# Layer 3 of a decoder: the mixture's routing moved from a phase of its own into the rounds of the cross attention before it

## The reference, cut to what matters

```python
x = x + jnp.tanh(g_xattn[3]) * _L3_xattn_ref(_layernorm(x, axis=-1), ctx_2048, ...)
x = x + jnp.tanh(g_ffn[3]) * _L3_ffn_ref(_layernorm(x, axis=-1), L3_ffn_Wg, L3_ffn_w1, L3_ffn_w2)

def _moe_forward(x, Wg, w1, w2):            # S = 4096 tokens, E = 8 experts, K = 2, C = 1280
    probs = jax.nn.softmax(xr @ Wg, axis=-1)
    gate_vals, expert_idx = jax.lax.top_k(probs, K)
    flat_e = expert_idx.reshape(-1)
    oh = jax.nn.one_hot(flat_e, E, dtype=jnp.int32)
    pos = jnp.sum((jnp.cumsum(oh, axis=0) - 1) * oh, axis=1)   # rank of a choice within its expert
    kept = pos < C
    ...                                     # rows gathered per expert, relu(x w1) w2, weighted sum
```

## Time and profile before

| | us |
|---|---|
| median of 3 runs (lowest, highest) | 3552.48 (3547.12, 3557.26) |
| the profiled execution: time | 3538.33 |
| the profiled execution: span | 3536.3 |
| mean granted TensorE clock, share of full | 0.898 |
| PE, DVE, ACT, POOL busy | 2850.8, 2150.4, 1478.8, 1097.6 |

### The profile page before, as it was taken

How to read it: one execution, slowest core, us unless ns; L and a number is a source line. 1 busy time by engine, 2 the same in 40 slices (tenths; PEclk the granted TensorE clock), 3 DMA queues, 4 the chain that set the end, 5 groups by cost and what they waited for, 6 DMA issues and landing times. The chain is left out here.

```text
span 3536.3 us, 59953 instructions
## 1 busy us (share of the span) xinstructions
PE 2850.8 (81%) x20178; PEld 1824.3 (52%) x20178; DVE 2150.4 (61%) x4916; ACT 1478.8 (42%) x3032; POOL 1097.6 (31%) x1466
## 2 busy tenths in 40 slices
PE   5488887565899994679946798999989839999995
PEld 4233335222555553433323586454558628888884
DVE  7699995676677775734468686888868740000003
ACT  5377774254232224589935454222235302221120
POOL 3211111475233335412289442000034360111111
PEclk7599997798999997589969899999989759999997
DMA  8866644599422223678400341000034321211114
GB/s 270 202 115 120 122 100 141 212 363 344 138 82 81 78 81 138 165 140 117 86 1 1 136 145 58 1 1 1 1 117 143 103 74 37 77 60 57 57 58 146
DMA packets 261546, 386.11 MB, mean 109 GB/s; under 512 B 56801, under 2 KB 188878, under 8 KB 260992
## 3 DMA queue, kind: packets, MB, share of 16 engines
q1 hardware_dynamic: 226064, 301.49, 32.0%
q0 software_dynamic: 25152, 68.22, 5.6%
q10 hardware_dynamic: 10032, 12.58, 1.0%
HBM read 227.49 MB, written 160.24 MB: 110 GB/s over the span
## 5 line engine op out<-in xcount | busy, mean ns | idle before, releaser
L3090 POOL DMA_INDIRECT rows_out<-e_out,e_tr_dest x224 | 234.9, 1049 | 832.0 <-DVE e_out L3690 491.7
L1102 ACT ACTIVATE a_pt<-a_psS 128x512 f32<-128x512 f32 x512 | 277.6, 595 | 106.3 <-PE a_psS L998 101.9
L3690 DVE COPY e_out<-e_psD 128x512 f32<-128x512 f32 x40 | 27.7, 692 | 461.5 <-PE e_psD L3658 461.4
L3445 PE MATMUL e_psG<-e_wgu,e_yT 128*128 x576 | 276.3, 603 | 28.8 <-ACT e_yT L3477 26.3
L1124 DVE TENSOR_REDUCE a_mx_sb<-a_psM 128x4 f32<-128x1024 f32 x256 | 293.1, 1215 | 10.5 <-PE a_psM L981 9.5
L1012 PE MATMUL a_psV<-a_pt,a_vt 128*18 128x256 f32 x4096 | 290.2, 385 | 1.2 <-issue 0.8
L3647 PE MATMUL e_psH<-e_yT,e_w 128*128 128x256 f32 x1280 | 285.4, 381 | 1.6 <-issue 0.8
L3658 PE MATMUL e_psD<-e_w,e_hT 128*128 128x256 f32 x1280 | 282.7, 379 | 0.0
L3588 ACT ACTIVATE e_hT<-e_psH 128x512 f32<-128x512 f32 x160 | 95.5, 597 | 445.7 <-PE e_psH L3647 441.2
L3647 PEld LDWEIGHTS e_psH<-e_yT,e_w 128*128 128x128 f32 x1280 | 244.8, 191 | 35.8 <-issue 2.1
L3658 PEld LDWEIGHTS e_psD<-e_w,e_hT 128*128 128x128 f32 x1280 | 240.2, 190 | 31.1
(11 more groups left out here) (434 smaller groups left out, 6182.9 us busy)
## 6 DMA issues: line engine op xcount, KB each, us to landing
kbd<-e_wd SPq DMA_DIRECT2D x64, 512.0 KB
cr_kbd<-kbd SPq DMA_DIRECT2D x64, 512.0 KB, 3.7
rows_in<-zeros POOLq DMA_DIRECT2D x36, 522.0 KB, 6.4
e_xin<-rows_in SPq DMA_DIRECT2D x144, 128.0 KB
vbd<-e_bd SPq DMA_DIRECT2D x64, 272.0 KB
cr_vbd<-vbd SPq DMA_DIRECT2D x64, 272.0 KB, 2.7
cq_rows<-rows_out SPq DMA_DIRECT2D x32, 512.0 KB, 6.0
e_w<-in_L_ffn_w_dram SPq DMA_DIRECT2D x16, 1024.0 KB, 7.8
```

The costliest lines, as they stand in the source:

```text
L1102: act.activation(pt[:, probs(t, h), b, :, :], psS[:, unit(t, h, b) % S_BANKS, :].rearrange("p (k c) -> p k c", k=KC), ACT.Exp, scale=scale ...
L3090: pool.indirect_dma_start(out=self.rows_out[0:limit, :], out_offset=bass.IndirectOffsetOnAxis(ap=self.dest[:, t:t + 1], axis=0), in_=rows, ...
L3445: ins = pe.matmul(psG[:, u, :], yT[:, u, k, :], wgu[:, e, k, :], start=(k == 0), stop=(k == KC - 1))
```

## The change

`phase_route_scatter` is gone. Its work is a class `Routing3`, whose methods `phase_cross` calls inside its rounds, only in layer 3. Each step runs a fixed number of rounds behind: in round `s` tile s-5 is surveyed, s-9 normed, s-10 turned, s-11 routed; the group whose first tile is s-15 is chosen, with s-16 carried and counted, with s-17 placed; tile s-18 is scattered, 2 DMAs a round. The transposes go to the free columns of `psU`, the logits to `psT`, the counts to `psO`, so PE also waits for those who read or write these banks. The rounds run on to s = 49. The barrier between the phases, and the clearing of semaphores there, are gone; the setup of constants on POOL is in round 2, and the prefetch of expert weights is at tile 8 of the cross attention.

```diff
+class Routing3:
+    SURVEY, NORM, TURN, ROUTE = 5, 9, 10, 11
+    CHOOSE, CARRY, COUNT, PLACE, SEND = 15, 16, 16, 17, 18
...
+    def gpsimd(self, pool, s):
+        g = self.group_at(s, self.SURVEY + G - 1)
+        if g is not None:
+            pool.wait_ge(self.eased, g + 1)
+            pool.tensor_tensor(self.core.rstd[:, self.group(g)], self.vareps[:, self.group(g)], self.core.half[:, 0:G], ALU.pow).then_inc(self.rooted, 1)
+        t = self.tile_at(s, self.SEND)
+        if t is not None:
+            g, j = divmod(t, G)
+            pool.wait_ge(self.placed, g + 1)
+            for k in range(K):
+                pool.indirect_dma_start(out=self.rows_in[:, :], ...).then_inc(self.sent[g % self.RING], 16)
+    def turn(self, pe, s, psU, o_copied):
+        pe.wait_ge(self.y_ready, t + 1)
+        pe.wait_ge(o_copied, min(s - 2, TILES))
+        if t >= 1:
+            pe.wait_ge(self.y_copied, t)
+        for k in range(KC):
+            ins = pe.transpose(psU[:, DIM + k * P:DIM + (k + 1) * P], self.y[...], self.core.ident[:, :])
+    def count(self, pe, s, psO, o_ready):
+        pe.wait_ge(self.masked, g + 1)
+        pe.wait_ge(self.carried, (g + 1) * (G + 1))
+        pe.wait_ge(o_ready, min(s, TILES))
...
@@ phase_cross, tensor @@
-                for s in range(-4, TILES + 3):
+                for s in range(-4, TILES + 3 if routing is None else routing.last):
                     if ok(s + 1):
                         scores(s + 1)
                     if ok(s + 4):
+                            routing.logits_taken(pe, s)
                         turn_y(s + 4)
                     if ok(s):
                         turn_probs(s)
+                        routing.turn(pe, s, psU, o_copied)
                     if ok(s + 3):
                         project(s + 3)
                     if ok(s - 1):
+                            routing.ranks_taken(pe, s)
                         values(s - 1)
+                        routing.route(pe, s, psT, y_copied, sum_copied)
                     if ok(s + 2):
+                            routing.logits_taken(pe, s)
                         sum_squares(s + 2)
                     if ok(s - 2):
+                            routing.turned_out(pe, s)
                         turn_out(s - 2)
                     if ok(s - 3):
                         project_out(s - 3)
+                        routing.count(pe, s, psO, o_ready)
@@ flamingo_decoder @@
-        phase_cross(core, "cr3", kbd[1], vbd[1], turned[0], a["L3_xattn_b_q"], turned[3], a["L3_xattn_b_o"], x_gate(3))
-        core.clear_semaphores()
...
-            phase_route_scatter(core, a["L3_ffn_Wg"], weight, rows_in, 8 * CAPACITY, MARK3, f_gate(3), prefetch)
+            with ExitStack() as c2:
+                routing = Routing3(core, c2, a["L3_ffn_Wg"], weight, rows_in, 8 * CAPACITY, MARK3, f_gate(3), prefetch)
+                phase_cross(core, "cr3", ..., x_gate(3), routing=routing)
```

More of the change, by code:

```diff
@@ L1446, in phase_cross @@
+def phase_cross(core, name, kbd_dram, vbd_dram, wq, bq, wo, bo, gate, prefetch=None, routing=None):
     nc = core.nc
@@ L1518, in _ @@
                         prefetch(sp)
+                    if t == 8 and routing is not None:
+                        routing.sync(sp)
                 load_values(TILES - 2)
@@ L1524, in _ @@
                 pool.memset(ones[:, :], 1.0).then_inc(ones_made, 1)
-                for s in range(-6, TILES + 1):
+                for s in range(-6, TILES + 1 if routing is None else routing.last):
                     t = s + 6
@@ L1651, in _ @@
                     if ok(s + 4):
+                        if routing is not None:
+                            routing.logits_taken(pe, s)
                         turn_y(s + 4)
@@ L1681, in _ @@
                             act.activation(pT[:, t % 2, 4 * r:4 * r + 4, :], psP[:, r, :, :], ACT.Copy).then_inc(p_copied, 1)
+                    if routing is not None:
+                        routing.scalar_turned(act, s, psU)
                     t = s + 1
@@ L1696, in _ @@
                         act.activation(square[:, t:t + 1], psT[:, 1, 0:1], ACT.Copy).then_inc(sum_copied, 1)
+                    if routing is not None:
+                        routing.scalar_logits(act, s, psT, q_summed)
                     t = s - 2
@@ L1707, in _ @@
                 dve.tensor_scalar(bias_out[:, :], bias_out[:, :], gate, None, ALU.mult).then_inc(bias_scaled, 1)
-                for s in range(-6, TILES + 4):
+                for s in range(-6, TILES + 4 if routing is None else routing.last):
+                    if routing is not None:
+                        routing.vector_survey(dve, s, added)
                     if ok(s + 6):
@@ L1721, in _ @@
                         dve.bn_aggr(core.mv[:, t, :], stats[:, t % 2, :]).then_inc(averaged, 1)
+                    if routing is not None:
+                        routing.vector_average(dve, s)
+                        routing.vector_multiply(dve, s, psO)
                     if ok(s + 1):
@@ L1748, in _ @@
                                           ALU.subtract, ALU.mult).then_inc(y_ready, 1)
+                    if routing is not None:
+                        routing.vector(dve, s)
                     if ok(s - 1):
```

474 lines of the change are left out of this document (251 added, 223 removed).

## The result

| | us |
|---|---|
| before, median of 4 runs beside it (lowest, highest) | 3550.3 (3547.12, 3557.26) |
| changed, median of 4 runs | 3507.6 (3500.34, 3513.66) |
| ratio, 95% interval | 0.9878, [0.9861, 0.9895] |
| changed, profiled execution: time, span, mean clock | 3507.26, 3505.5, 0.902 |
| predicted | 3505 (3484 to 3546) |

A forecast was written before the change was run, and what follows sets the result against it. DVE was to bound the attention's rounds, POOL's scatters what follows. Of 119.7 us, 27 for longer rounds and 45 behind the attention leave 47.7 gained: 3552.5 - 47.7 = 3504.8, predicted 3505, range 3484 to 3546.

The forecast's parts named there:

- The bound of the rounds: Layer 3 cross attention: PE's round grows from 5.6 to 6.4 us, DVE's mean to 6.71, so DVE becomes the bound.
- DVE's 6.9 us a round: Rounds 15 to 28: 6.9 us each, between DVE's mean 6.71 and worst round 8.2; 18.5 us added over 14 rounds.
- the stretch: Attention's rounds 5 to 33 together: 27 us longer with the routing inside; lower bound 15, upper 45.
- The clock: PE's clock in the attention's rounds with routing inside: stays at 1.00.
- The rival of the falling clock: Waits lower PE's clock in the rounds: about 11 us each, 57 us more, ending at 3562; chance 0.03.
- Rounds 29 to 34: End of the attention, worked as rounds 29 to 33 with two `place`, one `choose`, one `carry_on`: 5.5 us longer.
- POOL in the rounds: From round 18 two scatters a round, 2.56 us, fit in the 2.66 us that POOL idles.
- The tail: From round 34's output projection to the last scatter's end: 45 us, between 41 and 46, upper bound 50.
- the starving of POOL: Behind the attention POOL may wait for group 5's `place`; DVE's 8.6 us a group otherwise keeps ahead of 10.2 of scatters.
- Late steps in the rounds: Rival: scatters in rounds 18 to 33 delay hand-overs and `place`, 64 us more, ending at 3569; chance 0.11.
- Waits adding up: Rival: DVE's group work adds to PE's rounds, about 8.3 us each in 15 to 28, ending at 3530; chance 0.19.
- The rule on the shared port: DVE steps sharing ports with GpSimd could wait out a scatter; predicted norm at worst 0.25 us late, sum unchanged.

The follow-up runs named there:

- experiments 3: Changed kernel with DVE's norm for the router done twice, the second into a spare tile; one run, 3527.9 us.
- experiment 4: Changed kernel with the two transposes per tile for the router done twice on PE; one run, 3518.9 us.
- experiment 5: Changed kernel repeated (3505.6 us); variants of it: count in `psT` instead of the output bank 3504.4, norm on ACT instead of DVE 3495.8, both 3500.8.
- experiment 2: Changed kernel without the 32 scatters of groups 4 to 7, those after the attention; one run, 3485.6 us.
- experiment 1: Changed kernel without the 32 scatters of groups 0 to 3, those beside the attention's rounds; one run, 3504.4 us.
- experiment 6: Changed kernel with scatters of groups 4 to 7 dropping all rows but index 0 (3505.2 us), or replaced by chained memsets (3494.4 us); one run each.

## Why the prediction was right, and where its terms were off

*The bound of the rounds.* Right. PE's round without DVE in the way came out at 6.34 us where 6.4 was worked out (rounds 11 to 14: 25.36, forecast 4 x 6.3), and the doubled transposes cost 0.22 a round there. The logits' four records took 0.61 us from first start to last end, not 0.45, and the round did not show it. That DVE, not PE, would be the bound from round 15 on is right only in part: PE was the busier of the two, and without the clock's share 4.5 us more on DVE cost 3.3 and 3.0 us more on PE cost 1.6 (experiments 3 and 4).

*DVE's 6.9 us a round.* Measured 7.17; the stretch 100.3 us, forecast 14 x 6.9 = 96.6. Of the 3.7 us between them 2.7 are the half-clock round. Without it a round is 6.97 us: DVE's own sum was 6.49, below the 6.71 of the working, and the waits took 0.48 over it where 0.2 had been given, so two misses nearly cancel. The working had named the place, the count that waits for the division of its own round; experiment 5 prices it at 2.0 us over fourteen rounds, besides the clock. (In the working, 14 x (6.9 - 5.6) is 18.2 and not 18.5, and a round of before is 79.20 / 14 = 5.66 us there; neither moves the sum by more than 1 us.)

*The clock.* Forecast 1.00 throughout. Measured 0.97, with round 25 partly at the 1.2 GHz level and 2.7 us longer for it. The prediction had named a clock that leaves 1.00 before round 34 as a sign of being wrong, and this sign came true. The rival of the falling clock was right in kind for one round of fourteen and wrong in size: 2.7 us, not 57. The Trainium skill's rule on waits between bursts ("TensorE: Matmul & The Clock Gate", HAM oscillation) is drawn from longer waits, for a DMA, that let the clock drop each time. The trace agrees with it in that a wait was followed by a fall, and not in "each time": the three other counts of the changed kernel, which waited 0.39 to 1.07 us, kept the full clock, and so did one of 1.30 us in experiment 2.

*Rounds 29 to 34.* 24.8 against 17.7 before, +7.1, forecast +5.5. With rounds 11 to 14 (25.4 against 22.7) and 15 to 28 (100.3 against 79.2) the stretch cost 31.2 and not 27.

*POOL in the rounds.* Right: two scatters a round fit, and experiment 1 shows them to be free. The first was issued at 2733.13, in POOL's round 18, while PE was in round 19.

*The tail.* Forecast 45, measured 49.8. The 32 x 1.28 = 41.0 and the root's 1.1 came as worked out. The step that was mis-sized is the starving of POOL: 3.44 + 4.93 = 8.4 us where about 3 had been left. The prediction said that DVE keeps ahead "unless its steps are hindered"; they were: the first time by the attention's last add, 3.7 us late, the second by a chain of late steps. Without late scatters group 6 is placed at 17.3 us, long before POOL is done with group 5 at 24.6; with them at 28.6. The tail is where the mechanism of the earlier trace rows lives, and the upper bound of 50 held, just.

*The rivals.* Late steps in the rounds: refuted by experiment 1. Waits adding up: 0.27 us a round over the forecast and not 1.4, and most of the 0.27 is the clock. The sum was 3504.8, the time 3507.6. The terms were 9 us too hopeful in the profiles (4.2 in the stretch, 4.8 in the tail: 38.7 gained, not 47.7). In the medians 42.7 was gained; the 4 us between this and the profiled 38.7 are within the spread of the runs, so the closeness of the total is in part luck. So is the base: the forecast starts from 3552.5 us, and before measured 3550.3 beside the changed kernel, which hides 2.2 of the 5.0 us by which the gain fell short.

*The rule on the shared port.* In rounds and tail the norm took 382 ns at the least, 409 in the median, 667 at the most, and 384, 407 and 412 in experiment 2 behind the last scatter; a scatter takes 0.97 us, so none was waited out. Beside memsets on GpSimd it took 832 in the mean (experiment 6). The Trainium skill's rule of a shared port pair ("SBUF — State Buffer", Who interferes with whom), by which the operation issued first holds the pair for its whole length, agrees with the trace beside memsets, and does not beside scatters.

## What to carry to other kernels

Before moving work into another loop's idle time, make the sum for each engine, and then look at the waits that the moved work puts into the program order: an engine with 6.5 us of work in a 6.3 us round cost 7.2, and the cheapest cure was to take 0.4 us off that engine, giving it to one that idled. A wait of 1.0 to 1.3 us cost another 1.5 to 2.9 us by the clock of the round after it, once in each of five profiles of the same rounds, and its length didn't tell which one. And where indirect transfers go out back to back, give no dependent chain of small steps to the same stretch: it becomes half again as long.

## What the runs showed of the hardware that was not expected

While indirect scatters went out back to back on GpSimd, in rows of 8 to 16, hand-overs between TensorE, VectorE and ScalarE started up to 3.7 us after what they waited for had ended, and the chain behind the attention took 35 us instead of 24. Where the row began only as the attention's last add fell due (experiment 1), that add was on time. Two scatters in a row, then a pause, delayed nothing. Dropping nearly all rows did not help (34.6 us); memsets of about that length (1.03 us) caused no late starts, but doubled VectorE's norm from 402 to 832 ns.

The same rounds lost 1.5 us to the half clock in two profiles and 2.7 to 2.9 in three, behind counts that had waited 1.01 to 1.29 us, while a count that had waited 1.30 kept the full clock. Where the counts waited 0.94 us or less (experiment 4, and the three variants of experiment 5) none of these rounds ran at half clock.
